# Reciprocals ahead of output parts, and a new place for evictions, maxima and a store, in a two-layer attention chain

## What is computed

```python
hidden = concatenate([context, x])            # 512 + 256 rows per batch
q, k, v = x @ Wq, hidden @ Wk, hidden @ Wv
scores = einsum('bqhgd,bkhd->bhgqk', q, k) * scale
attn = softmax(scores)                         # over 768 columns
out = einsum('bhgqk,bkhd->bqhgd', attn, v)
x = x + tanh(gate) * (out @ Wo)
```

## Time and profile before

| | us |
|---|---|
| median of 3 runs | 1265.38 |
| lowest and highest run | 1257.82, 1265.85 |
| the profiled execution | 1258.08 |
| its span | 1256.3 |
| TensorE busy in the span | 1182.3 |
| VectorE busy | 909.4 |
| ScalarE busy | 637.6 |
| GpSimd busy | 517.5 |

### The profile page before, as it was taken

The page is one execution under the profiler, slowest core; times in us unless marked ns, Lnnn a source line. Parts: engine busy times, 40 slices in busy tenths (PEclk is TensorE's granted clock), DMA queues, the critical chain, the costliest instruction groups (busy, mean ns, idle before and its releaser), DMA issues.

```text
span 1256.3 us, 19440 instructions
## 1 busy us (share of the span) xinstructions
PE 1182.3 (94%) x7154; PEld 927.8 (74%) x7154; DVE 909.4 (72%) x1748; ACT 637.6 (51%) x1046; POOL 517.5 (41%) x385
## 2 busy tenths in 40 slices
PE   6999999999999998999989999997899998999986
PEld 5878888878888876777878879886775444777733
DVE  6589888886798798874677976897557773442287
ACT  3466556645566555641355644565146777232252
POOL 5126365625236377534242724234634002265212
PEclk9999999999999999999999999999999999999999
DMA  5588869975689597850386956878131000572000
GB/s 193 104 157 162 170 140 179 181 142 107 137 157 185 123 179 137 158 136 22 72 167 109 219 97 120 165 132 174 37 123 25 1 2 1 166 168 76 1 1 34
DMA packets 356238, 146.39 MB, mean 117 GB/s; under 512 B 327793, under 2 KB 334097, under 8 KB 356145
## 3 DMA queue, kind: packets, MB, share of 16 engines
q1 hardware_dynamic: 356144, 145.15, 55.3%
HBM read 57.17 MB, written 5.37 MB: 50 GB/s over the span
## 4 chain that ended last, share of the span: by engine, by line
PE 48%; DVE 9%; ACT 2%; POOL 2%; issue 2%; DMA 1%; SPq 0%; DVEq 0%; ACTq 0%; POOLq 0%
PE ps L876 6%; PE ps L2018 5%; PE ps L904 4%; PE ps L843 4%; PE ps L1584 3%; PE ps L1610 3%; DVE p L1166 3%; DVE rows_and_turned L1152 3%; PE ps L828 2%; PE ps L2031 2%; PE ps L819 2%; PE ps L805 2%; PE ps L2316 2%; PE ps L1566 1%; PE ps L1595 1%
## 5 line engine op out<-in xcount | busy, mean ns | idle before, releaser
L1000 ACT ACTIVATE ps<-ps,rows_and_turned 128x768 f32<-128x768 f32 x192 | 168.1, 875 | 201.5 <-DVE rows_and_turned L1152 201.5
L876 PE MATMUL ps<-kT,qT 128*128 128x512 f32 (+3 forms) x1152 | 238.9, 343 | 27.8 <-DVE p L1166 26.3
L876 PEld LDWEIGHTS ps<-kT,qT 128*128 128x128 f32 (+1 forms) x1152 | 199.2, 189 | 83.0 <-DVE p L1166 29.7
L1008 ACT ACTIVATE p<-ps,rows_and_turned 128x768 f16<-128x768 f32 x192 | 173.0, 901 | 125.2 <-ACT ps L1000 114.3
L904 PE MATMUL ps<-pT,vv 128*128 128x256 f16 (+1 forms) x1728 | 221.7, 274 | 6.2 <-issue 6.2
L1152 DVE TENSOR_REDUCE rows_and_turned<-ps 128x1 f32<-128x768 f32 x192 | 183.1, 954 | 56.8 <-PE ps L876 54.9
L1166 DVE SCALAR_TENSOR_TENSOR p<-ps,rows_and_turned,p 128x768 f16<-128x768 f32 (+2 forms) x256 | 201.4, 808 | 3.7 <-ACT p L1008 3.7
L904 PEld LDWEIGHTS ps<-pT,vv 128*128 128x128 f16 (+1 forms) x1728 | 167.3, 107 | 26.5 <-issue 9.6
L828 PE MATMUL ps<-xT,wq 128*128 128x512 f32 x528 | 144.0, 408 | 0.0
L737 POOL TENSOR_TENSOR wo<-raw,one 128x512 fp32r<-128x512 f32 (+1 forms) x48 | 50.8, 1058 | 225.2 <-PE ps L843 199.4
L1942 POOL TENSOR_TENSOR f2w<-f2raw,f2w 128x1024 fp32r<-128x1024 f32 (+2 forms) x33 | 52.6, 1622 | 149.2 <-ACT f2w L2062 149.2
(11 more groups left out here) (277 smaller groups left out, 1913.9 us busy)
## 6 DMA issues: line engine op xcount, KB each, us to landing
raw<-in_l_wq SPq DMA_DIRECT2D x44, 256.0 KB, 3.3
f2raw<-in_f_w SPq DMA_DIRECT2D x11, 776.0 KB, 5.0
rows_and_turned<-in_m_w SPq DMA_DIRECT2D x11, 768.0 KB, 5.6
raw<-in_l_wo SPq DMA_DIRECT2D x32, 256.0 KB, 3.3
pT<-p SPq DMA_TRANSPOSE x192, 3.7
raw<-in_l_wo SPq DMA_DIRECT2D x16, 192.0 KB, 3.3
w3gu<-rows_and_turned SPq DMA_DIRECT2D x11, 256.0 KB, 2.8
ctxraw<-in_ctxT SPq DMA_DIRECT2D x2, 1024.0 KB, 8.0
```

The source lines that it names most:

```text
L876: last = nc.tensor.matmul(sc[:, lo:hi], query(A, h, qp)[:, r * P:(r + 1) * P], keys(A, h // A.g)[0:hd, kp, b, lo:hi], start=(qp, kp) == PA ...
L1000: nc.scalar.activation(score_banks(n), score_banks(n), ACT.Exp, bias=nmax[:, n % 32:n % 32 + 1], accum_out=rsum[:, n % 32:n % 32 + 1]).the ...
L1008: nc.scalar.activation(p16[:, n % 3, HI], score_banks(n), ACT.Copy, scale=rden[:, n % 32:n % 32 + 1]).then_inc(sem("att_half"), 1)
```

## The change

It has five parts.

1. `denominator(n)` comes directly behind the remainder in every step, ahead of the output part and of the evictions.
2. The last value part of a group (V05, V25) is a last job and no longer an inner one.
3. `A.soon`: a value part is evicted early only if its bank is taken by an inner or a last job of the step, and no longer always. For a query it is still the inner jobs alone that count.
4. The block maxima come two steps earlier; for near tiles the first part stays and the second moves to the step after it.
5. The stores of the last tile of layer 1 come two steps later.

```diff
@@ -101,8 +101,8 @@
                 inner[at].append(("K", u, c))
         for u in range(0, kv, 2):
             n, v = RT * self.g * u, [("V", u, c) for c in range(6)]
-            places = ((last, 0), (inner, 2), (last, 2), (inner, 3), (last, 3), (inner, 4)) if u == 0 else (
-                (inner, n + 3), (last, n + 3), (inner, n + 4), (inner, n + 5), (last, n + 5), (inner, n + 6))
+            places = ((last, 0), (inner, 2), (last, 2), (inner, 3), (last, 3), (last, 4)) if u == 0 else (
+                (inner, n + 3), (last, n + 3), (inner, n + 4), (inner, n + 5), (last, n + 5), (last, n + 6))
             for (which, at), job in zip(places, v):
                 which[at].append(job)
         for h in range(heads):
@@ -171,9 +171,10 @@
             else:
                 used[b] = self.place[j]
         self.soon = {}
-        for (_, _, before_it), (n, inner_jobs, _) in zip(self.steps, self.steps[1:]):
+        for (_, _, before_it), (n, inner_jobs, last_jobs) in zip(self.steps, self.steps[1:]):
             taken = [self.bank[j] for j in inner_jobs] + ([4] if n in self.scale_steps else [])
-            self.soon[n] = [j for j in before_it if j[0] in "OV" or (j[0] == "Q" and self.bank[j] in taken)]
+            wanted = {"O": range(8), "V": taken + [self.bank[j] for j in last_jobs], "Q": taken}
+            self.soon[n] = [j for j in before_it if self.bank[j] in wanted.get(j[0], ())]
         self.hi_place = {j: i + 1 for i, j in enumerate(j for j in order if j[0] != "O")}
 
 
@@ -199,9 +200,9 @@
             n = first_tile + i
             near = i and tiles[i - 1] == h - 2
             for part in range(2):
-                self.amax_at[RT * h + 2 + part + (2 - part if near else 0), part] = n
+                self.amax_at[RT * h + part + (4 if near else 0), part] = n
                 self.scale_at[RT * h + 6 + 2 * part, part], self.step_at[RT * h + 9 + part, part] = n, n
-            self.load_weights_at[RT * (tiles[i - 1] if i else h - 4) + 9], self.store_at[RT * h + 16] = n, n
+            self.load_weights_at[RT * (tiles[i - 1] if i else h - 4) + 9], self.store_at[RT * h + (18 if before and i + 1 == len(tiles) else 16)] = n, n
             o = self.stream.index(("o", h + 1, 0))
             q = next((k for k in range(o + 1, len(self.stream)) if self.stream[k][0] == "q"), o + 2)
             self.round_after[self.stream[o]], self.round_after[self.stream[q]] = (n, 0), (n, 2)
@@ -1186,15 +1187,13 @@
                     value_scale_spread(0)
                 elif 1 <= n <= A.items:
                     remainders(n - 1)
+                if n < A.items:
+                    denominator(n)
                 if n >= LAG + 2 and (n - LAG) % 2 == 0:
                     outputs((n - LAG - 2) // 2)
-                if n == 1:
-                    denominator(n)
                 for what in ended:
                     if what not in soon:
                         job(what)
-                if 1 < n < A.items or n == 0:
-                    denominator(n)
                 for what in inner:
                     job(what)
                 ended = end
```

## The result

The changed kernel takes 1271.88 us (median of 10 runs, 1266.51 to 1276.69), the kernel before 1260.62 (10 runs, 1256.2 to 1265.85). The ratio is 1.0085, with a 95% interval of 1.0064 to 1.0106: slower by 8 to 13 us, most likely by 10.7 (0.0085 of 1260.6), and just short of 1% (timed again on another chip, in experiment 5, it was 1.0111, 1.0084 to 1.0139). The profiled execution took 1271.73 us, 13.7 more than that of before. The forecast said 1269.5, with a range that holds the result. But its sum was +4.1, from a median of three runs (1265.38) that ten runs put at 1260.62. So the time came out near partly by luck: a base 4.8 too high and a rise too small by about 7 nearly cancel, and the rise was forecast at less than half.

The account below looks back on a forecast made before the run. TensorE, busy 94% of the 1256.3 us span, paces the attention layers, so only its gaps can change the time. The terms sum to +4.1 us, which on the 1265.4 median gives 1269.5 us, range 1258 to 1278.

Parts of the forecast that it names:

- Term 1: Step 4: V05 waits for Q20's eviction, now behind the reciprocal; +2.2 us in layer 0, +2.5 in layer 1.
- Rival A: The stall of step 4 does not show, being early enough or swallowed by a later gap: 1264 us, chance 0.14.
- Term 2: TensorE's granted clock falling behind the new gaps at step 4 in both layers: +0.9 us, ends -0.8 and +2.6.
- Term 3: Block maxima two steps earlier: +1.4 us in layer 1 (0 to 3), -0.9 in layer 0 (-1.5 to 0).
- Term 5: Last store two steps later frees SyncE's queue and ends TensorE's gap near 863: -2.2 us (-2.3 to -0.8).
- Term 4: Layer 1: V25 behind the weighted values no longer waits 0.37 for V24's eviction: -0.4 us.
- Term 6: Reciprocal directly behind the remainder: -0.3 us from earlier halves at layer ends, +0.9 from VectorE waiting for the exponential.
- Rival B: VectorE becomes the bound, paying 0.14 in each of 95 steps: +16.5 us, 1282 us, chance 0.09.
- The checks: Expected profile: V05 waiting about 3 us, smaller gaps, no store wait, ScalarE idle about 90, VectorE idle 10 to 15 more.
- one sign of being wrong: Scores waiting for VectorE's remainders in many more than 28 places would show the forecast wrong, in favour of Rival B.
- Rival C: ScalarE's halves pace the steps, so the quarter of their idle time expected to go wins 31 us: 1238, chance 0.04.

Follow-up runs that it names:

- experiment 5: Whole change plus 18, then 13, unread TensorE products ahead of V05 at step 4: 1.0072, 1.0053 to before; the unaltered change timed again beside the latter: 1.0111.
- 13 unread products: Whole change, with TensorE writing 13 products nobody reads into a free bank ahead of V05 at step 4, both layers: 1267.86 us, 1.0053 to before.
- experiment 8: Whole change, but V05 stays among the inner jobs of step 4 as before: 1263.15 us, 1.0022 to the kernel before.
- experiment 1: Whole change, but a query half is also evicted early when a last job takes its bank: 1261.68 us, 1.0008 to the kernel before.
- experiment 6: Kernel of experiment 1 with the reciprocal back where it was before the change: 1255.26 us, 0.9952 to the kernel before.
- experiment 9: Kernel of experiment 6 with the block maxima back where they were before the change: 1257.84 us, 0.9976 to the kernel before.
- experiment 4: Kernel before with only the last store of rounded weights of the first attention layer two steps later: 1258.04 us, 0.9975.

## Why the forecast was right in its sign and wrong in its size

| term of the forecast | forecast | traces | runs |
|---|---|---|---|
| 1 stall, both layers | +4.7 | 2.6 + 2.7 | +3.9 to +5.7 |
| 2 clock | +0.9 | +4.5, then +0.8 | +4.0 to +7.9 (falls elsewhere included) |
| 3 maxima | +0.5 | -0.5, -3.0 (half of it clock) | -2.0, -3.0 |
| 4 V25 | -0.4 | -0.2 | not tried |
| 5 store | -2.2 | -2.2, -2.6 | -3.2 |
| 6 reciprocal | +0.6 | +8.8 (up to step 59 of layer 1) | +6.9, +7.1 |

- **Term 1** held in place, engine, order and size. The wait of V05 was put at 3.2 and is 3.05, and the gap of step 6 fell to 0.98 as said. In the traces (13 unread products, the clock full) layer 0 loses 1.75 against before, and 0.86 more against an execution of the same code whose clock did not fall there; layer 1 loses 2.67. By the runs it is the distance of the 13 unread products from experiments 8 and 1: 0.0031 and 0.0045 of 1260. Rival A needed this stall to vanish without the edit of experiment 1, and it stood there in all four places in which it was looked at.
- **Term 2** failed. The step said: "I take back 0.8 for the present fall and put 1.7 on each new gap with a chance of one half", since "a stretch of 3.4 us at half clock costs at most 1.7 us of work". That bound came from one fall in the trace of before, and took its length as the longest there is. In the first profile the clock fell in both layers, in layer 1 for ten microseconds on end: jumps of 3.2 and 6.6 less 1.75 and 2.67 are 5.4, less the 0.86 of before, 4.5. In the second it was 0.0 and 1.6 in the same way. The rule that I cited from the Trainium skill ("TensorE: Matmul & The Clock Gate", "HAM oscillation — how this bites in real kernels"), which gives it for waits mostly longer than these, pointed to the larger price at both gaps. The first profile agrees, the second in one layer of two.
- **Term 3** was too high in layer 1, though inside its bounds (0 to 3): the steps do start up to 1.2 later there, but the next steps give nearly all of it back, and 0.25 stays where I wrote 1.4. "In the step after it TensorE has a query half again, and its scores (718.29) start some 0.5 later" was taken as the end of the recovery; it goes on for three steps. Step 60 of layer 0 gave 1.0, for 0.9 forecast. Of the -3.0 between experiments 6 and 9, about 1.5 arises in steps 111 to 113 of layer 0, where the clock is 0.50 in the trace of experiment 9 and 1.00 in that of 6.
- **Term 5** held. **Term 4** has its sign; the gap closed by 0.22 of the 0.37, and no run tried it alone.
- **Term 6** failed by a factor of ten, and it is the largest error. Two sentences did it. "The scaling starts at 529.95, 0.14 later" measures from the end of one row to the start of the next; from start to start it is 0.21, and a step without slack grows by 0.23. And "perhaps six to eight steps reach TensorE" was a guess, where a count was to be had: in 30 steps of layer 0 VectorE does block maxima or the step of a w3 tile and goes into its next maximum without idle time in the trace of before, and each of them pays in full. Rival B had this mechanism, but the wrong steps and price (0.14 in 95, not 0.23 in 30). Its sign of the many waits came true; "The 94% of TensorE speaks against it" was no argument, since a share of the span says nothing of the steps in which VectorE is full.
- The checks: ScalarE's 90, VectorE's 12.3, V05's wait, the gaps and the store all came as written. So did one sign of being wrong: 45 waits for remainders where 28 were. What the list lacked was a check on the creep, for instance that the maxima of steps 10 to 50 stand at a constant distance from those of before.
- Rival C: the halves' idle time fell by 34.6 us and nothing of it was won; in the reciprocal-only kernel it fell by 32.1 (to 93.1), and the time rose by 6.9.

The parts add up within the measurement: 6.9-2.0-3.2 = +1.7 for the single edits, where experiment 1 has +1.0. It holds these three, and V05 and V25 as last jobs besides, which no run tried alone; the table gives them some -1.5 at step 4 of layer 0 and -0.6 at step 4 of layer 1. With the 9.7 us that the change lies over experiment 1 the single edits come to +11.4, for +10.7 measured. Each of these terms is uncertain by about 2 us.

Open is how the clock's share splits between the two layers on average; two profiles show 1.5 and 3.9, then 0 and 1.6.

## What to carry to other kernels

If the order of an engine's queue is set by a rule, an edit of one job can silently drop another out of the rule. Look for the evictions that the next job of TensorE needs, and see whether each is still early. An instruction that waits even 0.2 us costs that in each step in which its engine has no slack. So look for the steps in which it goes into the next one without idle time, count them by the kind of their work, and price them from start to start; don't share out an average. To move a producer ahead is only worth it when someone waits for it.

## What was not expected of the hardware

The granted clock does not follow from the wait alone. In the trace of before the clock was 0.52 from 60.0 to 63.4, behind a gap of 2.03. The kernel of experiment 4 has the same instructions there, and the same gap. First its timeline, then the same stretch of its windows:

```profile
59.97 1.31 PE L876 MATMUL ps<-kT,qT 128*128 128x512 f32 x6 [2.03 <-DVE p L1166]
```

```profile
60.00:63.40 3.40, 2.42 (x16) 1.89 (x17) 2.26 (x5) 1.92 (x4) 2.31 (x2) 1.00 0.75 134
```

The clock is 1.00, and from then on it runs 0.86 us ahead of before. In the changed kernel a wait of 3.05 us cost layer 0 1.5 us of clock in one profile and nothing in the other. Layer 1 had half clock over 10 us once, and for V05 alone the second time. Single profiles of one program thus differ by over 4 us from such falls alone (table, first two columns: 13.68 and 8.81 at step 7 of layer 1), and with 13 unread products in the wait the clock held in both layers of the one profile that there is.
